# First attention of a two-layer gated decoder: turns by DMA, masks as rows of the keys, three buffers, all steps written out, routing's tables at its end

## The chip, the cores and the metric

The kernel runs on one core of a Trainium2 chip. The metric is the device time of one execution in microseconds; less is better. The core has TensorE (matmuls and the loading of their weights), VectorE, ScalarE, GpSimd and SP, which here only issues transfers, and 16 DMA engines. The profile calls them PE, DVE, ACT, POOL and SP.

## The reference

32 sequences of 256 tokens with 256 channels pass two layers. Each is a gated cross-attention to 120 context rows and a gated feed-forward part; the first layer's is a mixture of 8 experts with the best 2 per token.

```python
x = x + jnp.tanh(g_xattn[0]) * _L0_xattn_ref(_layernorm(x, axis=-1), ctx_1024, L0_xattn_Wq, L0_xattn_Wkv, L0_xattn_Wo, L0_xattn_bo)
x = x + jnp.tanh(g_ffn[0]) * _L0_ffn_ref(_layernorm(x, axis=-1), L0_ffn_w_router, L0_ffn_w1, L0_ffn_w2, L0_ffn_w3)
...
            q = _apply_rope(q)
            k = _apply_rope(k)
            attn = jnp.einsum('bhqd,bhkd->bhqk', q, k) * scale
            attn = jax.nn.softmax(attn, axis=-1)
            out = jnp.einsum('bhqk,bhkd->bhqd', attn, v)
            out = out.transpose(0, 2, 1, 3).reshape(B, Nq, C)
            return out @ Wo + bo
...
        scores = jax.nn.softmax(xf @ w_router.T, axis=-1)
        expert_weights, expert_indices = jax.lax.top_k(scores, K)
        h = jax.nn.silu(jnp.einsum('td,edh->eth', xf, w1)) * jnp.einsum('td,edh->eth', xf, w3)
        y = jnp.einsum('eth,ehd->etd', h, w2)
```

There are 16 heads of 16 channels. The second layer has an attention with layer norms and a gate, and a ternary feed-forward part with a short convolution; the change doesn't touch them.

## The kernel before, in words

Four stages run one after the other, each a block in which every engine has its own program: `attention_first`, which also routes tokens to experts, `experts`, `attention_second` and `ternary_ffn`. Between blocks all engines meet.

`attention_first` takes one sequence (a batch) per step, in a software pipeline: in step n an engine works on batch n - s for the stage s of each piece, and the pieces of a step stand in an order written out by hand. `filled` writes 12 steps out, loops over two steps at a time for the other 20, and writes the drain of 10 steps out. Engines tell each other of progress by semaphores with named steps (`Signal`, `wait`); `freed` waits until a buffer's last reader is through.

A batch goes like this. SP loads xT, x and the context. TensorE makes queries (into `ps_c`) and keys and values (`ps_a`) from high and low halves in bf16. VectorE multiplies with the rotary tables, GpSimd adds (`qf`, `kf`), ScalarE and VectorE write high, high again and low halves side by side, 32 columns each for a pair of heads, into `qx` (two tiles of 128 tokens, 8 pairs, 96 columns) and `kx`. TensorE turns `kx` (L1044, 8 transposes into `ps_b`) and `qx` (L1095 and L1101, 16 into `ps_d` and `ps_b`). ScalarE copies them out: keys twice with a mask that keeps one head of the pair (`k2`, L540 and L543), queries as they are (`q2`, L567 and L569). TensorE then makes the scores of 128 queries to all keys four heads at a time (`ps_m`, the names ms0 to ms7), VectorE takes each maximum (`mneg`), splits it in two halves (`mx`), TensorE turns it (L1086, into `ps_a`), ScalarE copies it (`mt`, L560), and VectorE copies it eight times into rows 96 to 127 of `q2` (L844). Rows 96 to 127 of `k2` hold one-hot rows, so that the score matmuls of the second kind (keys as rows, `ps_e`, sc0 to sc7) come out less the maximum. ScalarE takes the exponentials into `probs`, TensorE multiplies with the values (pv0, pv1), turns the result (tb, oT), VectorE divides, TensorE projects (`ps_b`), and VectorE adds the residual: `x1`, stored by SP.

Routing follows, on the same batch some steps later: norm (`e_xn`, L616, two buffers), a turn and the router's product in fp32, best two, a rank for each token by matmuls with a triangle and with ones, the slot number, and four scatters by GpSimd (L462, L499) of rows into `sent`. The copy of L616 waits until the scatters of the batch two earlier have landed.

The experts' weights are loaded in six pieces; ScalarE casts (`high`, L210) and VectorE subtracts (`low`, L216). Four pieces are done between steps 1 to 8 of `attention_first`, two at the start of `experts`.

`experts` begins with a count of tokens (L2110), VectorE's tables from it, and SP's eight stores of zeros behind each expert's rows (L1868); then SP loads rows by tiles of 256 (L1880), ScalarE and VectorE split them, a DMA transpose turns them (L1885, 128x1024 bf16), and TensorE starts (L2107).

## Time and profile before

| | us |
|---|---|
| median of 3 runs | 1959.78 |
| lowest, highest | 1959.65, 1960.63 |
| the profiled execution | 1951.88 |
| its span | 1950.1 |
| mean granted clock of TensorE in it | 0.959 of full speed |

All durations come from the profiled execution. Line numbers in the rows are those of the kernel before. Times of matmuls overlap their successors a little, so that the distance between starts tells more than a duration. Idle time in brackets names who ended it.

### The profile page before, as it was taken

The numbers are of one execution on the slowest core, as the hardware profiler recorded it, in microseconds if no ns is written. First come the engines' busy times: TensorE is split into PE (matmuls) and PEld (weight loads), VectorE is DVE, ScalarE is ACT, GpSimd is POOL, SyncE is SP. The second block draws the span as 40 slices with busy tenths as digits, with TensorE's granted clock in tenths as the row PEclk, the third lists the DMA queues.
The fourth block names the chain that finished last, engine by engine and source line by source line (L and its number), as shares of the span: only waits on it lengthen the run. The fifth ranks groups of instructions, "written<-read, shape, count | busy, mean of one in ns | idle before, by whom it ended". The sixth has DMA issues, their size and how long they took to land. (4 is left out here: it accounts for less than half of the span.)

```text
span 1950.1 us, 52076 instructions
## 1 busy us (share of the span) xinstructions
PE 1707.9 (88%) x15841; PEld 1433.9 (74%) x15841; DVE 1489.0 (76%) x4340; ACT 1418.6 (73%) x2824; POOL 1003.7 (51%) x1295
## 2 busy tenths in 40 slices
PE   4989999999719999999975999999999578888887
PEld 3667888888518999999963888888887366666666
DVE  4879999999534354433325999999998699999996
ACT  6888999999524454444424777777777499999997
POOL 3448888888622333333337667666661233333332
PEclk8899999999959999999987999999999799999999
DMA  5434343342229675555524555555541112211111
GB/s 177 162 106 151 114 129 114 119 130 87 89 96 218 146 135 143 138 137 138 139 74 94 109 127 112 119 117 118 123 111 53 62 55 65 65 62 59 61 59 51
DMA packets 265532, 212.75 MB, mean 109 GB/s; under 512 B 108160, under 2 KB 255104, under 8 KB 264384
## 3 DMA queue, kind: packets, MB, share of 16 engines
q1 hardware_dynamic: 240832, 176.50, 32.3%
q0 software_dynamic: 24576, 34.62, 8.6%
q8 instruction: 75, 1.23, 0.3%
...
## 5 line engine op out<-in xcount | busy, mean ns | idle before, releaser
L2107 PE MATMUL e_ps_ab<-e_turned,k_w_hi 128*128 128x256 bf16 (+1 forms) x1704 | 285.1, 274 | 21.6 <-DMA e_turned<-e_rows 21.6
L1929 POOL TENSOR_TENSOR e_h_lo<-e_h 128x256 bf16<-128x256 f32 (+1 forms) x213 | 139.0, 653 | 303.4 <-DVE e_h L2046 303.4
L2046 DVE TENSOR_TENSOR e_h<-e_s,e_ps_ab 128x256 f32<-128x256 f32 (+1 forms) x213 | 88.2, 415 | 227.6 <-ACT e_s L1954 227.6
L2107 PE MATMUL e_ps_ab<-e_turned,k_w_lo 128*128 128x256 bf16 (+1 forms) x852 | 233.1, 274 | 0.0
L2107 PEld LDWEIGHTS e_ps_ab<-e_turned,k_w_hi 128*128 (+1 forms) x1704 | 177.6, 107 | 36.3 <-issue 21.7
L1954 ACT ACTIVATE e_s<-e_ps_ab 128x256 f32<-128x256 f32 (+1 forms) x213 | 81.1, 382 | 123.9 <-PE e_ps_ab L2107 122.9
L2489 PE MATMUL f_ps_h<-f_qh,p_arena 128*128 128x256 bf16 x512 | 122.8, 279 | 35.5 <-DVE f_ql L2453 28.2
L1961 ACT ACTIVATE e_yo<-e_ps_y,e_xe 128x256 f32<-128x256 f32 x142 | 59.5, 470 | 112.7 <-PE e_ps_y L2107 112.7
L2489 PE MATMUL f_ps_h<-f_ql,p_arena 128*128 128x256 bf16 x512 | 122.0, 278 | 0.0
L2107 PE MATMUL e_ps_y<-e_w_hi,e_h 128*128 (+1 forms) x426 | 116.5, 273 | 0.0
L1289 POOL DMA_INDIRECT a_xa<-back_rows,a_where x64 | 107.9, 1686 | 15.7 <-issue 15.2
L2107 PE MATMUL e_ps_y<-e_w_hi,e_h_lo 128*128 (+1 forms) x426 | 115.9, 272 | 0.0
L2107 PE MATMUL e_ps_y<-e_w_lo,e_h 128*128 (+1 forms) x426 | 115.7, 272 | 0.0
L2267 POOL TENSOR_TENSOR f_y<-f_y,f_tmp 128x510 f32<-128x510 f32 x32 | 43.6, 1362 | 136.6 <-DVE f_y L2388 136.6
L1299 POOL DMA_INDIRECT a_xa<-back_rows,a_where x64 | 100.4, 1568 | 21.4 <-issue 21.0
L2107 PEld LDWEIGHTS e_ps_ab<-e_turned,k_w_lo 128*128 (+1 forms) x852 | 90.7, 107 | 7.0
L2489 PEld LDWEIGHTS f_ps_h<-f_qh,p_arena 128*128 128x128 bf16 x512 | 50.7, 99 | 61.4 <-DVE f_ql L2453 35.9
L2039 DVE TENSOR_TENSOR e_rows<-e_xe,e_rows 128x256 bf16<-128x256 f32 x142 | 78.2, 589 | 19.4 <-ACT e_rows L1948 19.1
L499 POOL DMA_INDIRECT sent_rows<-k_xn,k_slot x64 | 71.2, 1112 | 18.6 <-issue 18.6
L506 POOL TENSOR_TENSOR a_qf<-p_arena 128x512 f32<-128x512 f32 x32 | 40.7, 1273 | 62.8 <-DVE p_arena L674 62.8
L462 POOL DMA_INDIRECT sent_rows<-k_xn,k_slot x64 | 64.0, 1000 | 17.0 <-issue 17.0
L889 PE MATMUL a_ps_b<-a_wo,a_ot 128*128 128x256 f32 x256 | 64.6, 398 | 0.6 <-ACT a_ot L578 0.6
(429 smaller groups left out, 6421.7 us busy)
## 6 DMA issues: line engine op xcount, KB each, us to landing
...
```

What stands on the lines that cost most here:

```text
L462: nc.gpsimd.indirect_dma_start(sent[:, :], bass.IndirectOffsetOnAxis(ap=slot[:, b.par, t, 0:1], axis=0), e_xn[:, b.par, t, :], None).then_ ...
L499: nc.gpsimd.indirect_dma_start(sent[:, :], bass.IndirectOffsetOnAxis(ap=slot[:, b.par, t, 1:2], axis=0), e_xn[:, b.par, t, :], None).then_ ...
L889: last = nc.tensor.matmul(dst, l, r, start=(n == 0), stop=(n == len(terms) - 1))
L1289: nc.gpsimd.indirect_dma_start(xa[:, b.par, t, :], None, y_rows[:, :], bass.IndirectOffsetOnAxis(ap=where[:, b.par, 2 * t + 1:2 * t + 2], ...
L1299: nc.gpsimd.indirect_dma_start(xa[:, b.par, t, :], None, y_rows[:, :], bass.IndirectOffsetOnAxis(ap=where[:, b.par, 2 * t + 0:2 * t + 1], ...
L1929: nc.gpsimd.tensor_tensor(h_lo[0:k, b.par, c, :], h[0:k, b.par, c, :], h_hi[0:k, b.par, c, :], ALU.subtract).then_inc(mg.sem, 1)
L1954: nc.scalar.activation(s[0:k, b.par, c, :], ps_ab[0:k, bank(b, c), 0:N], ACT.Silu).then_inc(ma.sem, 1)
L1961: nc.scalar.activation(yo[:, b.par, t, :], ps_y[:, b.par, t * D:(t + 1) * D], ACT.Copy, scale=xe[:, b.n % XE, t, D:D + 1]).then_inc(my.sem, 1)
L2039: last = nc.vector.tensor_tensor(rows_[:, b.n % XR, 1, :, t, :], xe[:, b.n % XE, t, 0:D].rearrange("p (k n) -> p k n", k=KC), rows_[:, b.n ...
L2046: nc.vector.tensor_tensor(h[0:k, b.par, c, :], s[0:k, b.par, c, :], ps_ab[0:k, bank(b, c), N:2 * N], ALU.mult).then_inc(mh.sem, 1)
L2107: last = nc.tensor.matmul(to, left, right, start=(i == 0), stop=(i == len(terms) - 1))
L2489: last = nc.tensor.matmul(dst, l, r, start=(n == 0), stop=(n == len(terms) - 1))
```

## The change

- `unrolled` writes all 45 steps out (14 stages), with `Staged` for the waits, whose values are constants.
- `kx` and `qx` become 128 columns wide per head and per pair. Each head's keys are written to their own columns, the other head's stay zero, and the one-hot part is stored once in columns 96 to 127 (`own`). SP turns them with one DMA transpose each per batch (128x2048 bf16) straight into `k2` and `q2`, which get three buffers; `v1` too. The transposes on TensorE, ScalarE's four copies out of them and the masks are gone.
- The maxima are spread into `q2` by a DMA from SP (`m_ld`) instead of VectorE's copy.
- `e_xn`, `slot` and `pair` have four buffers.
- The four pieces of weights of `attention_first` are cast and subtracted in steps 32 to 36.
- The count, the tables and the stores of zeros stand at the end of `attention_first`; SP and ScalarE issue four stores each. `experts` no longer has them.
- The order of each engine's pieces is another. GpSimd's operations are the same.

The diff, cut to its core:

```diff
+def arrived(eng, sems, batch, parts=1):
+
+    if batch is not None:
+        eng.wait_ge(sems[batch.n % len(sems)], 16 * parts * (batch.n // len(sems) + 1))
...
-        self.slot = sb("slot", [P, 2, NT, 2], mybir.dt.int32)
+        self.xn = sb("xn", [P, 4, NT, WIDE])
+        self.slot = sb("slot", [P, 4, NT, 2], mybir.dt.int32)
...
+class Staged:
+
+
+
+    def __init__(self, sem, steps):
+        self.sem = sem
+        self.steps = [(name, int(stage)) for name, stage in (s.split(":") for s in steps.split())]
+        assert len(set(self.steps)) == len(self.steps)
+
+    def value(self, n, step):
+
+        names = [name for name, _stage in self.steps]
+        place = names.index(step)
+        when = n + self.steps[place][1]
+        return sum(min(B, max(0, when - stage + (i <= place))) for i, (_name, stage) in enumerate(self.steps))
+
+    def wait(self, eng, batch, step):
+
+        if batch is not None:
+            eng.wait_ge(self.sem, self.value(batch.n, step))
...
+def unrolled(step, stages, also):
 
 
     def at(n):
-        return lambda s: Batch(n - s, (n - s) // 2, (n - s) % 2) if 0 <= n - s < B else None
-
-    def within(batch):
-        return lambda s: batch.back(s) if s else batch
-
-    for n in range(fixed):
+        return lambda s: Batch(n - s, (n - s) // 2, (n - s) % 2, (n - s) // 4, (n - s) % 4) if 0 <= n - s < B else None
+
+    for n in range(B + stages - 1):
         step(at(n))
         also(n)
-    with eng.Fori(0, (B - fixed) // 2) as k:
-        step(within(Batch(2 * k + fixed, k + fixed // 2, 0)))
-        step(within(Batch(2 * k + fixed + 1, k + fixed // 2, 1)))
...
         xt = pre.arena[:, 5120:6144].rearrange("p (t k n) -> p t k n", t=2, k=KC)
-        qx = sb("qx", [P, NT, NP, 96], BF16)
-        kx = sb("kx", [P, NP, 96], BF16)
-        q2 = sb("q2", [P, 2, NP, N], BF16)
-        k2 = sb("k2", [P, 2, H, S], BF16)
-        v1 = sb("v1", [P, 2, H, VW], F32)
...
+        qx = sb("qx", [P, NP, NT, P], BF16)
+        kx = sb("kx", [P, H, P], BF16)
+        q2 = sb("q2", [P, 3, NP, N], BF16)
+        k2 = sb("k2", [P, 3, H, P], BF16)
+        v1 = sb("v1", [P, 3, H, VW], F32)
...
+        def pad(eng, first, stop):
+
+            sh.s_tab.wait(eng, once, "padding")
+            for e in range(first, stop):
+                at = eng.value_load(sh.padding[0:1, e:e + 1], min_val=0, max_val=E * ROOM - ROWS)
+                eng.dma_start(sent[bass.ds(at, ROWS), :].rearrange("(t p) d -> p t d", p=P), sh.zeros[:, :, :]).then_inc(sh.s_pad, 16)
+
...
+        def own(at):
+
+            rows_ = kx[0:S, :, :]
+            return bass.AP(rows_.tensor, rows_.offset + at, [rows_.ap[0], [2 * P, NP], [P + HD, 2], [1, HD]])
...
+                if b is not None:
+                    act1.wait(sp, b, "k_hi2")
+                    dve1.wait(sp, b, "k_lo")
+                    nc.sync.dma_start_transpose(k2[:, b.n % 3, :, :], kx[:, :, :].rearrange("p h k -> p (h k)")).then_inc(k_ld[b.n % 3], 16)
...
+                if b is not None:
+                    act6.wait(sp, b, "mt")
+                    nc.sync.dma_start(q2[96:128, b.n % 3, :, :], mt[:, :].unsqueeze(1).to_broadcast([2 * H, NP, N])).then_inc(m_ld[b.n % 3], 16)
...
+                    act1.wait(sp, b, "q_hi2")
+                    dve1.wait(sp, b, "q_lo")
+                    nc.sync.dma_start_transpose(q2[:, b.n % 3, :, :].rearrange("p c (t n) -> p (c t) n", t=NT),
+                                                qx[:, :, :, :].rearrange("p c t k -> p (c t k)")).then_inc(q_ld[b.n % 3], 16)
...
-                if n in (4, 5):
-                    sh.load(sp, a, n - 2)
+                if n in (33, 34):
+                    sh.load(sp, a, n - 31)
                 if n == 6:
                     for j in range(SPARE // ROWS):
                         at = E * ROOM + j * ROWS
                         sp.dma_start(sent[at:at + ROWS, :].rearrange("(t p) d -> p t d", p=P), sh.zeros[:, :, :]).then_inc(sh.s_spare, 16)
-                if n in (9, 10):
-                    sh.load(sp, a, n - 5)
+                if n in (37, 38):
+                    sh.load(sp, a, n - 33)
+                if n == STAGES + LAST - 1:
+                    pad(sp, 0, E // 2)
...
+                    arrived(act, k_ld, at(5))
+                    nc.scalar.activation(own(0), kf[0:S, :].rearrange("p (c j d) -> p c j d", j=2, d=HD), ACT.Copy).then_inc(act1.sem, 1)
...
+                    dve7.wait(act, b, "enm")
+                    arrived(act, e_sent[1], at(14), NT)
...
-                if n in (1, 2):
-                    sh.high(nc, n - 1, sh.flat[0])
-                if n in (6, 7):
-                    sh.high(nc, n - 4, sh.flat[1])
+                if n in (32, 33):
+                    sh.high(nc, n - 32, sh.flat[0])
+                if n in (35, 36):
+                    sh.high(nc, n - 33, sh.flat[1])
+                if n == STAGES + LAST - 1:
+                    pad(act, E // 2, E)
...
-                    nc.vector.tensor_copy(q2[96:128, b.par, :, :], mt[:, :].unsqueeze(1).to_broadcast([2 * H, NP, N])).then_inc(dve2.sem, 1)
...
-                if n in (2, 3):
-                    sh.low(nc, n - 2, sh.flat[0])
-                if n in (7, 8):
-                    sh.low(nc, n - 5, sh.flat[1])
+                if n in (32, 33):
+                    sh.low(nc, n - 32, sh.flat[0])
+                if n in (35, 36):
+                    sh.low(nc, n - 33, sh.flat[1])
+                if n == LAST + 11:
+                    tables()
...
+                    arrived(pe, k_ld, b)
+                    arrived(pe, q_ld, b)
+                    for j in range(2):
+                        last = nc.tensor.matmul(ps_m[:, 1, j * 2 * S:(j + 1) * 2 * S].rearrange("p (j s) -> p j s", s=S), q2[0:96, b.n % 3, 2 + j, 0 * P:1 * P],
+                                                k2[0:96, b.n % 3, 4 + 2 * j:6 + 2 * j, 0:S],
+                                                start=True, stop=True)
...
+                if n == LAST + 13:
+                    gp2.wait(pe, final, "eseen")
+                    dve5.wait(pe, final, "top2")
+                    nc.tensor.matmul(ps_m[:, 0, 0:E], ones[:, :], seen[:, :], start=True, stop=True).then_inc(sh.s_count, 1)
+
...
-            s_tab.wait(sp, once, "padding")
-            for e in range(E):
-                at = sp.value_load(padding[0:1, e:e + 1], min_val=0, max_val=E * ROOM - ROWS)
-                sp.dma_start(block_of(at), zeros[:, :, :]).then_inc(s_pad, 16)
             s_tab.wait(sp, once, "row")
             sp.wait_ge(sh.s_spare, 16 * (SPARE // ROWS))
-            sp.wait_ge(s_pad, 16 * E)
+            sp.wait_ge(sh.s_pad, 16 * E)
             for k in range(2):
-                for par in range(2):
-                    sp.wait_ge(sh.sent[k][par], 16 * NT * (B // 2))
+                for quad in range(4):
+                    sp.wait_ge(sh.sent[k][quad], 16 * NT * (B // 4))
```

TensorE, steady step, before: the turn of the maxima (L1086), the turns of queries (L1095, L1101), keys and values, then the scores less the maximum (L1114).

```order
428 L1086 MATMUL a_ps_a<-a_identb,a_mx 32x128 x2
429 L1095 MATMUL a_ps_d<-a_identb,a_qx 96x128 x8
430 L1101 MATMUL a_ps_b<-a_identb,a_qx 96x128 x8
431 L889 MATMUL a_ps_a<-a_wkvh,a_ch 120x512
432 L889 MATMUL a_ps_a<-a_wkvl,a_ch 120x512
433 L889 MATMUL a_ps_a<-a_wkvh,a_cl 120x512
434 L889 MATMUL a_ps_a<-a_wkvh,a_ch 120x512
435 L889 MATMUL a_ps_a<-a_wkvl,a_ch 120x512
436 L889 MATMUL a_ps_a<-a_wkvh,a_cl 120x512
437 L1114 MATMUL a_ps_e<-a_q,a_k 120x256 x2
```

TensorE, steady step, of the change: the same turn (L1143), the first two pairs of maxima of the next batch (L1150, L1162) around the context's turn, keys and values, the rank, the projection (`a_wo`), and the scores (L996).

```order
1417 L1143 MATMUL a_ps_a<-a_identb,a_mx 32x128 [waits a0_act1,a0_dve5]
1418 L1143 MATMUL a_ps_a<-a_identb,a_mx 32x128
1419 L1150 MATMUL a_ps_m<-a_k,a_q 128x240 [waits a0_q_ld0,a0_k_ld0]
1420 L1150 MATMUL a_ps_m<-a_k,a_q 128x240
1421 L973 MATMUL a_ps_d<-k_ident,a_of 128x128 [waits a0_dve7]
1422 L973 MATMUL a_ps_d<-k_ident,a_of 128x128 x3
1423 L1162 MATMUL a_ps_m<-a_k,a_q 128x240 x2
1424 L963 MATMUL a_ps_a<-a_wkvh,a_ch 120x512 [waits a0_act6,a0_gp2]
```

```order
1433 L1179 MATMUL a_ps_c<-k_seen,k_ones 128x8 x2
1434 L963 MATMUL a_ps_b<-a_wo,a_ot 128x256 [waits a0_act6]
1435 L963 MATMUL a_ps_b<-a_wo,a_ot 128x256 x3
1436 L996 MATMUL a_ps_e<-a_q,a_k 120x256 [waits a0_act6,a0_m_ld2]
1437 L996 MATMUL a_ps_e<-a_q,a_k 120x256
```

The query turns are gone, and between the turn of the maxima and the scores that need it stand more products than before, with a wait for the spreading transfer (`m_ld`) at the scores and one for both turns (`q_ld`, `k_ld`) at L1150.

SP, steady step, before: store of x1, slots, then the four loads.

```order
94 L414 DMA x_rows<-a_x 128x2x256
95 L57 ISA
96 L398 ISA
97 L398 DMA slots<-k_slot 128x4
98 L57 ISA
99 L402 ISA
100 L402 DMA p_arena<-in_xT 128x512
101 L57 ISA
102 L404 DMA a_xa<-in_x 128x2x256
103 L57 REGISTER_ALU
```

SP, steady step, of the change, from the spread of the maxima (L449) to the next one.

```order
228 L449 DMA a_q<-a_mt 32x8x256
229 L453 DMA x_rows<-a_x 128x2x256
230 L458 DMA_TRANSPOSE a_q<-a_qx 128x16x128
231 L463 DMA p_arena<-in_xT 128x512
232 L467 DMA slots<-k_slot 128x4
233 L433 DMA_TRANSPOSE a_k<-a_kx 128x16x128
234 L437 DMA a_xr<-in_x 128x2x256
235 L441 DMA a_xa<-in_x 128x2x256
236 L445 DMA a_ca<-in_ctxT 128x240
237 L449 DMA a_q<-a_mt 32x8x256
```

Three transfers have come in among the six, two of them turns, and register and branch instructions are gone.

## Rows read from the trace of the kernel before

**Rows 1.** By stretch: us, busy us of PE, PEld, DVE, ACT, POOL, clock, DMA share, GB/s.

```profile
540.00:600.00 60.00, 17.35 (x119) 14.79 (x120) 22.41 (x70) 14.64 (x25) 15.34 (x25) 0.56 0.41 112
420.09:434.43 14.34, 14.34 (x147) 11.59 (x146) 13.74 (x55) 14.05 (x29) 11.97 (x17) 1.00 0.39 115
```

**Rows 2.** Timeline of TensorE, one step: start us, us, engine, line, operation, tiles, count.

```profile
420.09 0.29 PE L1086 MATMUL a_ps_a<-a_identb,a_mx 128*32 128x128 bf16 x2
420.30 0.65 PE L1095 MATMUL a_ps_d<-a_identb,a_qx 128*96 128x128 bf16 x8
...
421.23 0.38 PE L889 MATMUL a_ps_a<-a_wkvh,a_ch 128*120 128x512 bf16 x1
...
422.53 0.38 PE L1114 MATMUL a_ps_e<-a_q,a_k 128*120 128x256 bf16 x2
...
426.15 1.90 PE L889 MATMUL a_ps_b<-a_wo,a_ot 128*128 128x256 f32 x8
...
429.45 0.58 PE L1044 MATMUL a_ps_b<-a_identb,a_kx 120*96 120x120 bf16 x8
429.94 0.38 PE L1050 MATMUL a_ps_m<-a_k,a_q 96*128 96x240 bf16 x2
```

**Rows 3.** Timeline of TensorE, the turn of the maxima: first, ninth, last batch.

```profile
43.23 0.27 PE L1086 MATMUL a_ps_a<-a_identb,a_mx 128*32 128x128 bf16 x2
...
176.35 0.28 PE L1086 MATMUL a_ps_a<-a_identb,a_mx 128*32 128x128 bf16 x2
...
503.36 0.28 PE L1086 MATMUL a_ps_a<-a_identb,a_mx 128*32 128x128 bf16 x2
```

**Rows 4.** Groups by line, 300 to 400 us: busy us, mean ns | idle before.

```profile
L540 ACT ACTIVATE a_k<-a_ps_b,a_pairmask 96x960 bf16<-96x960 bf16 x7 | 7.5, 1073 | 0.0
L567 ACT ACTIVATE a_q<-a_ps_d 96x1024 bf16<-96x1024 bf16 x7 | 7.0, 1000 | 0.0
L560 ACT ACTIVATE a_mt<-a_ps_a 32x256 bf16<-32x256 bf16 x7 | 2.6, 372 | 1.8 <-PE a_ps_a L1086 1.8
L844 DVE COPY a_q<-a_mt 32x2048 bf16<-32x2048 bf16 x7 | 6.5, 926 | 3.0 <-ACT a_mt L560 3.0
L504 POOL TENSOR_TENSOR a_rstd<-a_ve,a_half 128x2 f32<-128x2 f32 x7 | 7.3, 1039 | 0.2
L479 POOL TENSOR_TENSOR a_e_rstd<-a_e_ve,a_half 128x2 f32<-128x2 f32 x7 | 5.1, 722 | 0.0
L499 POOL DMA_INDIRECT sent_rows<-k_xn,k_slot x14 | 15.8, 1129 | 3.3 <-issue 3.3
```

**Rows 5.** A stretch with one turn; a small transfer with its landing, 300 to 400 us.

```profile
818.00:820.00 2.00, 2.00 (x20) 1.78 (x19) 0.00 (x0) 0.84 (x2) 0.54 (x1) 1.00 0.72 139
...
slots<-k_slot SPq DMA_DIRECT2D x7, 2.0 KB, 1.7
```

**Rows 6.** The two lines that cast and subtract weights: ns min/median/max, first and last.

```profile
L210 ACT ACTIVATE k_w_hi<-k_w_f x4: 2533/2554/2602, 27.5 to 115.9; 128x2816 bf16<-128x2816 f32 x4
L210 ACT ACTIVATE e_w_hi<-k_w_f x2: 2746/2754/2763, 566.4 to 569.1; 128x3072 bf16<-128x3072 f32 x2
...
L216 DVE TENSOR_TENSOR k_w_lo<-k_w_f,k_w_hi x4: 3081/3358/4039, 47.2 to 147.0; 128x2816 bf16<-128x2816 f32 x4
```

**Rows 7.** The drain: ScalarE's group, then TensorE's and SP's timelines, with releasers.

```profile
L616 ACT ACTIVATE k_xn<-a_x,a_e_nmr,a_e_rstd 128x256 f32<-128x256 f32 x8 | 4.4, 592 | 15.0 <-DMA sent_rows<-k_xn,k_slot 15.0
...
566.46 0.17 PE L2110 MATMUL e_ps_y<-k_seen,k_ones 128*128 128x8 bf16 x1 [12.19 <-PEq L240]
588.26 0.61 PE L2107 MATMUL e_ps_ab<-e_turned,k_w_hi 128*128 128x256 bf16 x2 [21.63 <-DMA e_turned<-e_rows]
...
568.10 9.32 SPq L1868 DMA_DIRECT2D sent_rows<-k_zeros  x8
580.44 2.70 SPq L1880 DMA_DIRECT2D e_xe<-sent_rows  x3
584.91 1.36 SPq L1885 DMA_TRANSPOSE e_turned<-e_rows  x1
```

1207 lines of the change are left out of this document (575 added, 632 removed).

## The prediction

> **What bounds the kernel now.** I read the stages first: in the stretch from 540 to 600 us, between the first attention and the experts, TensorE is busy for 17.35 of 60 us at a mean granted clock of 0.56, while in one step of the first attention (420.09 to 434.43) it is busy for all of its 14.34 us at clock 1.00 [rows 1]. In that step ScalarE is busy for 14.05, VectorE for 13.74 and GpSimd for 11.97 us, and the DMA engines for 0.39 of it, 5.6 us [rows 1]. So the steady part is bound by TensorE, with two engines close behind, and the end of the stage is bound by waits.
>
> Next the timeline of TensorE over that step, from one turn of the maxima (L1086) to the next [rows 2]: there is no idle entry in it. Then the times of the same matmul for the first, ninth and last batch: 43.23, 176.35 and 503.36 [rows 3]. From the ninth on, 23 intervals take 327.0 us, 14.22 each; the first eight take 133.1, 16.6 each. The start is slower than the steady part although its steps hold less work.
>
> **The change, part by part.**
>
> *1. Turns by DMA: TensorE.* The 16 matmuls that turn queries begin at 420.30 and the next product begins at 421.23: 0.93 us. The 8 that turn keys take 429.45 to 429.94: 0.49 us [rows 2]. TensorE loses 1.42 us of 14.34, and nothing is added to it; its floor becomes **12.92 us** per step.
>
> *2. The other engines.* ScalarE loses four copies out of the turns (two of queries, 1.00 each, and two of keys with the mask, 1.07 each, of which one row each stands here): 4.1 us, so its floor is 14.05 - 4.1 = 9.9 [rows 1, 4]. VectorE loses the copy that spreads the maxima (L844), 0.93 us busy and 3.0/7 = 0.43 idle ahead of it [rows 4]: 13.74 - 0.93 = 12.81. GpSimd changes in order alone: 11.97 busy plus the pause ahead of its scatters, 3.3 us in 7 steps and the same for the second pair, 0.94 together: 12.91 [rows 1, 4]. Writing all steps out also removes the register instructions that the order of before shows between VectorE's operations; I price them at nothing, since VectorE's floor already lies under TensorE's.
>
> GpSimd's power on 128x2 (L504) takes 1.04 us where it starts beside VectorE's spreading copy, and the same shape elsewhere (L479) 0.72 [rows 4]. If the copy is what holds it, GpSimd's floor falls to 12.6. The Trainium skill (SBUF — State Buffer, "Who interferes with whom") says that a VectorE copy in a two-port mode and a GpSimd operation exclude each other for the whole instruction; by it the 0.3 us come back, without it they don't. The forecast doesn't need them.
>
> *3. What DMA gets.* In the experts' stage one turn of 128x1024 bf16 lies alone in a window of 2.00 us, with a DMA share of 0.72: 1.44 us of all 16 engines [rows 5]. The change issues two of 128x2048 per step, so 4 x 1.44 = 5.8 us. The spreading of the maxima (32 rows of 8 x 512 B, 128 KB) has no row; it is bounded below by nothing and above by a 128 KB turn, 0.7, and I take 0.5, near the turn since its pieces are small too. Sum: 5.6 + 5.8 + 0.5 = **11.9 us** of DMA work per step. That lies under 12.92, but it is 90% of it. The Trainium skill (DMA: Bandwidth & Descriptors, "Latency and other measured facts") gives 261 GB/s for DMA transposes; by it the two would take 4.0 us and the sum would be 10.1. The window gives 182 GB/s, and the sum goes by the window.
>
> SP waits in its order. Behind the maxima's spread stand the store of x1, the query turn, the next xT, the slots, the key turn and three loads; behind a query turn that waits for q_lo, all of the rest. The turns are asked for on TensorE one to two steps later and have three buffers, so only the spread is close to the path.
>
> *4. The spread.* Before: maxima turned, ScalarE copies, VectorE copies, scores. Now a transfer stands in VectorE's place. A 2 KB transfer takes 1.7 us from issue to landing here [rows 5]; I take 2.2 for 128 KB, bounds 1.7 to 4. With ScalarE's copy of 0.37 (L560) [rows 4] and two hand-overs of 0.1 the chain is 2.8 us after the turn. TensorE's work in between, by the new order and the times of [rows 2]: two maxima pairs 0.4, the context turn 0.4, keys and values 421.23 to 422.53 = 1.3, the projection about 1.7 (1.90 with the last one's tail): 3.9 us. So it is hidden with **1.1 us** to spare. With a landing of 4 us it would cost 0.7 per step.
>
> *5. The steady step.* Three floors of 12.92, 12.91 and 12.81 in one chain of waits won't meet without friction. Before, the second engine was at 98% and TensorE still had no gap. I take **13.2 us**, from 12.95 to 14.3 (the time of before, if DMA sets the pace).
>
> *6. The expert weights* (four casts of 2.55 us on ScalarE, four subtractions of 3.36 us on VectorE [rows 6]) leave steps 1 to 8 for steps 32 to 36. In the first eight intervals they hold 10.2 and 13.4 us of engines that are nearly full: taking both out at face value gives 133.1 - 23.6 = 109.5, and the shorter step 8 x 1.14 = 9.1 less: 100.4. **Gain 32.7** (bounds: 13.4 + 9 = 22 if only VectorE's count, 36). Two copies of masks at the very start go too, and two turns of longer latency stand in the first batch's way; I take these as equal. In steps 32 and 33 two subtractions lie in nearly full steps of VectorE: 6.7 us are paid there; the two at 35 and 36 fall into steps with no query work, and these are some 3 us shorter as they are now. The rest: 23 x 13.2 + 6.7 - 3 = 307.3 against 327.0. **Gain 19.7.**
>
> *7. The drain.* From the last turn of maxima (503.36) to the experts' first instruction (566.46) 63.1 us pass [rows 3, 7]. ScalarE's normalisation waits 15.0 us there for scattered rows whose two buffers are not free [rows 7]. With four buffers that wait has no cause; the spread's latency and the one more stage of scores cost 1 us. **Gain 14** (bounds 6, if GpSimd's four scatters a batch are next in line, to 22).
>
> *8. Tables and padding.* Now: count at 566.46, eight padding stores from 568.10 over 9.32 us, first load at 580.44, first turn at 584.91, first product at 588.26: 21.8 us [rows 7]. Afterwards count, tables and padding are done when the stage ends. What is late next are the last weights: two casts of 2.75 (to 5.5), then the second subtraction of 3.36 behind the first, 2.75 + 2 x 3.36 = 9.5 [rows 6], the rows' low half 0.8, and turn to product 588.26 - 584.91 = 3.35: 13.6. **Gain 8.2.** If the loads are late instead, up to 3 less. ScalarE and VectorE run the second half of these in before too, hidden by the wait for padding, whose cover is now gone.
>
> Sum: 32.7 + 19.7 + 14 + 8.2 = 74.6 us. The profiled execution took 1951.88 (span 1950.1), which gives 1877.3; the median of the three runs is 1959.78, 7.9 above it, and against that the forecast is **1885 us**.
>
> **The rivals.**
>
> *A. DMA or SP sets the pace.* 11.9 us of work at 90% leaves no room for bunching, and scatters of GpSimd share the engines. For it: the share is the highest in the kernel. Against it: all loads have a step's slack. Then the step is some 14.3: 31 x 1.1 = 34 more, 1919.
>
> *B. Slower than before: the turns are dear.* The new ones are twice as wide as the one measured. If a 128x2048 turn took longer than twice the 128x1024 one, the step would be 6.1 + twice that. The gain of 74.6 is gone at 74.6 / 31 = 2.4 us per step above 13.2, that is 4.8 us for a turn in place of 2.88. At 5.8 the step is 17.7 and the kernel takes 1885 + 31 x 4.5 = 2025. Against it: a wider turn is more blocks of the same size.
>
> *C. The floors are met and the drain collapses.* Step 12.95, drain gain 22: 1885 - 31 x 0.25 - 8 = 1869.
>
> *D. The start isn't shortened.* If the first steps were long from latencies and not from the weights, 22 us of the 32.7 stay: 1907. Against it: the intervals come down to 14.3 just when the weights are done.
>
> **How the numbers follow.** Forecast (1875 to 1900) 0.60; A 0.17; D 0.07; C 0.11; B 0.05. The range has to leave out at most 0.2: from **1865**, under C, to **1920**, which takes in D and A. About 0.2% (4 us) is what a measurement of this kernel can tell from no change. Faster by more than that: all but B and a worse A, **0.93**; within it 0.02; slower 0.05.
>
> **What would show it.** In the profile after: the interval between two turns of maxima in the steady part 13.0 to 13.6 and TensorE without idle entries there (parts 1, 5); ScalarE near 75% of it (2); DMA share near 0.9 in it (3); no wait of the scores for the transfer of maxima (4); the ninth turn of maxima near 143 and the last near 450 (6); last turn to the experts' first instruction near 49 (7); from there to the first product near 14 (8). Wrong would be: TensorE idle at each step for a_q or a_k from DMA (A, B), a turn's landing over 5 us, or a first product after 530.

## The result and the profile after

The changed kernel takes 1937.39 us (median; 1934.98 to 1938.79), the kernel before 1959.72 in the same comparison: a ratio of 0.9885 with a 95% interval of 0.9868 to 0.9902. It is faster by 22 us, where 75 were forecast, and the time lies above the range of 1865 to 1920. The profiled execution took 1934.98 us (span 1933.2) where the sum gave 1877.3.

First the places that the prediction's steps end at: the turn of the maxima (L1143 here, L1086 before) for the first, ninth and last batch, then the experts' first instruction and the first product. All rows are of the timeline of the changed kernel, and answer to [rows 3] and [rows 7].

```profile
45.48 0.40 PE L1143 MATMUL a_ps_a<-a_identb,a_mx 128*32 128x128 bf16 x2
...
149.96 0.29 PE L1143 MATMUL a_ps_a<-a_identb,a_mx 128*32 128x128 bf16 x2
...
496.55 0.28 PE L1143 MATMUL a_ps_a<-a_identb,a_mx 128*32 128x128 bf16 x2 [0.91 <-DVE a_mx L871]
...
557.19 2.76 ACT L229 ACTIVATE e_w_hi<-k_w_f 128x3072 bf16<-128x3072 f32 x1 [15.83 <-PEq L273]
...
570.53 0.61 PE L2115 MATMUL e_ps_ab<-e_turned,k_w_hi 128*128 128x256 bf16 x2 [29.35 <-DMA e_turned<-e_rows]
```

| Stretch | before | forecast | after | forecast missed by |
|---|---|---|---|---|
| to the first turn | 43.2 | 43.2 | 45.5 | 2.3 |
| first 8 intervals | 133.1 | 100.4 | 104.5 | 4.1 |
| other 23 intervals | 327.0 | 307.3 | 346.6 | 39.3 |
| last turn to the experts | 63.1 | 49.1 | 60.6 | 11.5 |
| experts' start to first product | 21.8 | 13.6 | 13.3 | -0.3 |
| first product to the end | 1361.8 | 1361.8 | 1362.7 | 0.9 |

So 39 of the 58 us are in the steady part, which was to become shorter by 20 us and became longer by 20; another 11.5 are in the drain. That the kernel is faster at all, as forecast, comes from the start (28.6 us) and from the experts' first product (8.5), not from the step.

The second view compares two steps of the changed kernel by windows (columns: length, then busy time and instructions of TensorE, its weight loads, VectorE, ScalarE, GpSimd, then the granted clock, the DMA share and GB/s). The first step lies ahead of the first scatter of rows, the second is one of the 19 alike (15.06 to 15.08 us); the last four of the 23 intervals take 18.15, 15.85, 13.37 and 12.95.

```profile
122.35:135.39 13.04, 13.04 (x123) 10.37 (x123) 13.00 (x54) 10.73 (x24) 9.55 (x15) 1.00 0.88 204
330.78:345.85 15.07, 13.60 (x123) 10.20 (x123) 14.61 (x55) 10.91 (x26) 11.66 (x17) 1.00 0.76 194
```

In the first, TensorE is busy throughout, in 13.04 us: within what part 5 forecast (13.2, from 12.95). In the second VectorE is busy for 14.61 us, 1.61 more, with the same instructions but one, and TensorE for 13.60 of 15.07. The DMA share is the lower one in the longer step. TensorE's longest wait in the second step, 0.7 us, is for VectorE's maxima, and none is for a transfer. So the step is VectorE's, and its groups by line for 300 to 400 us (busy us, mean ns, then the idle time ahead) name the instructions:

```profile
L789 DVE SCALAR_TENSOR_TENSOR a_pair<-a_e_ex,a_tg,a_e_rec 128x4 f32<-128x4 f32 x7 | 9.5, 1351 | 0.0
L809 DVE COPY k_xn<-a_pair 128x2 f32<-128x2 f32 x6 | 6.5, 1085 | 0.0
L890 DVE SCALAR_TENSOR_TENSOR a_qx<-a_qf,a_rstd,a_qx 128x256 bf16<-128x256 f32 x14 | 6.1, 474 | 0.0
```

Two instructions on 4 and 2 elements per partition lead the list, ahead of everything with 256 or 512 elements. The timelines of VectorE and of GpSimd, in the step ahead of the scatters (first three rows) and in a steady one (the others), show when they are long:

```profile
125.94 1.06 DVE L760 TENSOR_TENSOR a_kx<-a_kf,a_kx 120x256 bf16<-120x256 f32 x1
...
128.09 0.16 DVE L789 SCALAR_TENSOR_TENSOR a_pair<-a_e_ex,a_tg,a_e_rec 128x4 f32<-128x4 f32 x1
...
129.63 0.16 DVE L809 COPY k_xn<-a_pair 128x2 f32<-128x2 f32 x1
...
306.86 1.36 DVE L789 SCALAR_TENSOR_TENSOR a_pair<-a_e_ex,a_tg,a_e_rec 128x4 f32<-128x4 f32 x1
...
309.61 1.08 DVE L809 COPY k_xn<-a_pair 128x2 f32<-128x2 f32 x1
...
305.93 0.96 POOL L555 DMA_INDIRECT sent_rows<-k_xn,k_slot  x1 [0.30 <-issue]
306.91 1.29 POOL L560 TENSOR_TENSOR a_qf<-p_arena 128x512 f32<-128x512 f32 x1
...
309.50 1.16 POOL L512 TENSOR_TENSOR a_xl<-p_arena,a_xh 128x512 bf16<-128x512 f32 x1
```

`pair` ends (308.22) with GpSimd's addition `a_qf` (308.20), the copy (310.69) with GpSimd's subtraction `a_xl` (310.66). They cost 1.20 and 0.92 us more than alone, 2.12 together. VectorE's busy time grows by less, 1.61, mainly because `a_kx`, which takes 1.06 us beside `a_qf` in the step without scatters, takes 0.41 in the steady one: the 13.04 us hold such a meeting too, and that 2.12 lies so near to 15.07 - 13.04 = 2.03 is in part chance. Before the change the same `pair` took 0.20 us and the same copy 0.16. GpSimd's scatters shift its additions to this place: without them `a_qf` starts at 125.44, 2.65 us ahead of `pair`, and with them it follows the scatter of 305.93 at once. The meeting then comes back in each of the 19 steps.

The Trainium skill (SBUF — State Buffer, "Who interferes with whom") says that a VectorE instruction with two SBUF inputs contends with a GpSimd instruction that reads SBUF, that a copy in a two-port mode does too, that whoever comes second is fully blocked for the whole instruction, and that a reduction never contends on trn2. By that, a 0.16 us operation can cost the length of GpSimd's. The rows agree in that both end with GpSimd's operation. They don't show who came second: the record of `pair` begins 0.05 us ahead of that of `a_qf`. Experiments e1, e3 and e4 test the moment, e2 the kind of operation, and that for the copy alone: `pair` was moved but never exchanged.

### The profile page after: what moved, and what is told of

Its sections match the earlier page's. It is cut to its first block and busy times, and to the rows that moved or that the text cites. A ratio compares the mean times of both kernels' runs of the same rounds, so it can differ in the third digit from the quotient of the medians.

```text
span 1933.2 us, 48348 instructions
## 1 busy us (share of the span) xinstructions
PE 1676.1 (87%) x15073; PEld 1385.0 (72%) x15073; DVE 1508.7 (78%) x4308; ACT 1310.5 (68%) x2695; POOL 1000.9 (52%) x1297
## 5 line engine op out<-in xcount | busy, mean ns | idle before, releaser
L519 POOL DMA_INDIRECT sent_rows<-k_xn,k_slot x64 | 64.2, 1003 | 23.3 <-issue 23.0
L555 POOL DMA_INDIRECT sent_rows<-k_xn,k_slot x64 | 62.2, 973 | 19.7 <-issue 18.9
L2496 PE MATMUL f_ps_y<-p_arena,f_zq 128*128 128x256 bf16 x512 | 61.1, 273 | 1.2 <-ACT f_zq L2339 1.2
```

The source lines that it names most:

```text
L519: nc.gpsimd.indirect_dma_start(sent[:, :], bass.IndirectOffsetOnAxis(ap=slot[:, b.quad, t, 0:1], axis=0), e_xn[:, b.quad, t, :], None).the ...
L555: nc.gpsimd.indirect_dma_start(sent[:, :], bass.IndirectOffsetOnAxis(ap=slot[:, b.quad, t, 1:2], axis=0), e_xn[:, b.quad, t, :], None).the ...
L2496: last = nc.tensor.matmul(dst, l, r, start=(n == 0), stop=(n == len(terms) - 1))
```

## Experiments

The ratios are to before on the same chip. The step is the mean of the 18 intervals between the 10th and the 28th turn of maxima. The kernel before takes 1955.4, 1959.1, 1959.7, 1969.1 and 1970.3 us in the five sets of runs, the changed one 1937.4 and 1935.5 in the two that hold it. The step and first product of before are those of its one trace, of an execution of 1951.88 us.

| Kernel | step, us | ratio to before, or time | first product, us |
|---|---|---|---|
| before | 14.34 | 1 | 588.3 |
| changed | 15.07 | 0.9885; 0.9907 when repeated | 570.5; 571.0 |
| e1: `pair` elsewhere | 14.02 | 1920.6 of 1970.3 | 554.9 |
| e2: copy as reduction | 14.14 | 1923.4 of 1970.3 | 556.9 |
| e3: `pair` and copy elsewhere | 14.03 | 0.9729 | 549.3 |
| e4: before, copy elsewhere | 15.62 | 1983.8 of 1970.3 | 619.3 |
| e5: e3 and four value buffers | 13.81 | 0.9730 | 545.9 |
| e9: e5 and copies as reductions | 13.48 | 0.9744 | 540.7 |
| e11: e9 and a second store | 13.5 | 1906.9 of 1959.1 | 538.4 |

**e1: one instruction moved.** The edit, in VectorE's order:

```
 nc.vector.tensor_reduce(total[:, :], e_ex[:, :, :], AX_X, ALU.add)
+nc.vector.reciprocal(e_rec[:, :], total[:, :])
+nc.vector.scalar_tensor_tensor(pair[:, b.quad, :, :], ...)
 nc.vector.tensor_reduce(mneg[:, 0, 12:16], ...)
-nc.vector.reciprocal(e_rec[:, :], total[:, :])
 nc.vector.reciprocal(rsum[:, 1, :], ...)
-nc.vector.scalar_tensor_tensor(pair[:, b.quad, :, :], ...)
```

> The changed kernel with two of VectorE's routing instructions (the reciprocal e_rec and the weights' product pair, 128x4) in another place of VectorE's order: directly behind the sum total, where VectorE has an idle 0.45 us and GpSimd issues scatters. Nothing is added or left out. Theory (shared SBUF access): pair took 1.36 us beside GpSimd's 128x512 addition a_qf and 0.16 where nothing ran beside it; at the new place it takes 0.16 to 0.22, the step falls from 15.07 by up to 1.2, to 13.9 to 14.1, and the copy into k_xn stays at 1.0 to 1.1 if its phase stays. Rival 1 (DMA sets the pace of 15.07, its share being 0.80): the step stays at 15.0 to 15.1. Rival 2 (the lost time only moves to the next two-input operation that meets GpSimd): the step stays above 14.7 and another short VectorE operation takes over 1 us.

Measured: step 14.02, time 1920.6. The groups of VectorE for 300 to 400 us:

```profile
L780 DVE SCALAR_TENSOR_TENSOR a_pair<-a_e_ex,a_tg,a_e_rec 128x4 f32<-128x4 f32 x7 | 1.6, 223 | 0.2
L809 DVE COPY k_xn<-a_pair 128x2 f32<-128x2 f32 x8 | 1.4, 177 | 0.0
```

`pair` fell as expected, and the step with it. The copy fell too, which I had not expected: it wasn't moved, presumably since it now meets GpSimd at another moment; that was not tested. DMA as the pace (rival 1) is excluded: the same transfers now fit in 14.0 us.

**e2: same place, another operation.**

```
-nc.vector.tensor_copy(e_xn[:, b.quad, :, D:D + 1], pair[:, b.quad, :, 0:1])
+nc.vector.tensor_reduce(e_xn[:, b.quad, :, D:D + 1], pair[:, b.quad, :, 0:1], AX_X, ALU.add)
```

> The changed kernel with one instruction exchanged at its own place: the weight's copy into k_xn (128x2) that stands between two maxima (L809) is made by a reduction over one element instead of a copy; same input, same output, same order. Theory (the copy locks with GpSimd because of its access mode, a reduction doesn't): the instruction takes 0.16 us in place of 1.08, pair stays at 1.36, and the step falls by 0.9 to 14.1 to 14.3. Rival (any VectorE operation at that place waits, because of what it reads or because its turn comes late): it stays at 1.0 and the step at 15.07.

```profile
L789 DVE SCALAR_TENSOR_TENSOR a_pair<-a_e_ex,a_tg,a_e_rec 128x4 f32<-128x4 f32 x8 | 10.6, 1328 | 0.0
...
L809 DVE TENSOR_REDUCE k_xn<-a_pair 128x2 f32<-128x2 f32 x7 | 1.0, 139 | 0.0
```

At the same place of the order, with the same operands, the reduction takes 139 ns where the copy took 1085; `pair` is untouched at 1328. The step is 14.14, 0.93 shorter. So it is the kind of operation and not the place alone. That the copy runs in a two-port mode is the page's reason; no trace shows the mode.

**e3: both moved.** As e1, with the copy right behind `pair`.

> The changed kernel with the reciprocal e_rec, pair and the copy into k_xn all directly behind the sum total in VectorE's order. Nothing is added or left out. Theory: both long instructions fall to 0.16 to 0.22 us, VectorE's work per step to 12.9 and the step from 15.07 to 13.0 to 13.3; over the 22 steady intervals and some of the others this is 40 to 46 us, so the kernel takes 1890 to 1900 us against 1937.4 (0.965 to 0.970 of before). Rival 1 (DMA or SP sets the pace): 1930 to 1940. Rival 2 (the loss moves on): 1915 to 1935, with another VectorE operation over 1 us.

The ratio is 0.9729 (0.9713 to 0.9746); `pair` takes 222 and the copy 169 ns; the first product comes 21 us earlier. But the step is 14.03, as in e1, and not 13.0 to 13.3. The theory's cause holds, but it promised 2 us per step and got 1.04: the copy alone is worth 0.93 (e2) and both together hardly more, so that something else stands at 14.0. In the timelines of TensorE, VectorE and ScalarE in e3 another thing is late:

```profile
315.08 1.05 PE L1128 MATMUL a_ps_e<-p_arena,a_v 120*32 120x256 f32 x16
...
315.56 0.47 DVE L717 TENSOR_TENSOR a_k_sin<-a_ps_a,p_arena 120x128 f32<-120x128 f32 x2
...
317.15 0.38 ACT L597 ACTIVATE a_v<-a_ps_a 120x256 f32<-120x256 f32 x1 [2.23 <-PE a_ps_e L1128]
```

ScalarE's copy of the values waits for these two alone, the later of which ended at 316.13, and it starts 1.02 us after that. TensorE's turn of maxima waits for this copy.

**e4: the collision put into the kernel before.** The kernel before with its 0.16 us copy moved by one VectorE instruction:

```
-nc.vector.tensor_copy(e_xn[:, b.par, :, D:D + 1], pair[:, b.par, :, 0:1])
 nc.vector.tensor_tensor(k_cos[0:S, :], ps_a[0:S, 0:D], cos[0:S, 0, :], ALU.mult)
+nc.vector.tensor_copy(e_xn[:, b.par, :, D:D + 1], pair[:, b.par, :, 0:1])
 (the two products of k_sin)
```

> The kernel before with one instruction in another place: the weight's copy into k_xn (L853, 0.16 us, which starts at 351.36, just ahead of GpSimd's a_qf at 351.52 to 352.75) now stands behind the first product of the keys' rope, at about 351.76, inside a_qf. Nothing is added or left out. Theory (shared SBUF access): the copy takes 0.9 to 1.0 us, and since VectorE's 13.74 of 14.34 us become 14.5, the step grows from 14.22 to 14.4 to 14.8, the kernel by 4 to 15 us. Rival (the long copies of the changed kernel come from its DMA queues or from their place between maxima): the copy stays at 0.16 to 0.2 and the time within 2 us of before.

Its group for 300 to 400 us, then one step of it beside GpSimd's:

```profile
L865 DVE COPY k_xn<-a_pair 128x2 f32<-128x2 f32 x6 | 6.7, 1122 | 0.0
...
322.88 1.27 POOL L506 TENSOR_TENSOR a_qf<-p_arena 128x512 f32<-128x512 f32 x1 [0.59 <-DVE p_arena L674]
...
323.05 1.12 DVE L865 COPY k_xn<-a_pair 128x2 f32<-128x2 f32 x1
```

The long copy appears in a kernel that has none of the change: no DMA turns, two buffers, its own order. With one tiny copy 0.4 us later in the order the step is 1.28 us longer than in the trace of before, where I expected 0.2 to 0.6. Not all of that is the copy, whose excess is 0.96: `a_kx` (L744, two inputs in SBUF) takes 900 ns in e4 and 411 before, and ends with GpSimd's `a_e_ve`: it looks like a further meeting that the new phase brings. The size has a second caveat. The kernel is 13 us slower than before beside it (one run, above all seven of before, 1966.5 to 1972.3), but its first product comes 31 us later than in the trace of before, which is of an execution some 18 us faster than those seven. That the copy grows is shown; how much of 1.28 us is the move's is not. So the copy's part of the cause is shown from two sides: e2 by the kind of operation, e4 by the moment.

**e5: the wait for the values.** e3 with `v1` in four buffers, so that ScalarE waits for a product that is one batch older.

```
-v1 = sb("v1", [P, 3, H, VW], F32)
+v1 = sb("v1", [P, 4, H, VW], F32)
-pe9.wait(act, at(7), "pv1")
+pe9.wait(act, at(8), "pv1")
```

> The kernel of e3_both_early with four buffers for the values a_v in place of three, so that ScalarE's copy a_v (L597) waits for a product of values one batch older, long finished. Nothing is left out. In e3_both_early this copy starts 0.6 to 1.2 us after TensorE's last product of values and 0.8 to 1.5 after VectorE's k_sin, while in the short steps before 136 us it starts 0.07 after the product; the step there is 14.0 against 13.4. Theory (the wait for TensorE's product of values is what is late): the copy starts 0.1 us after k_sin, TensorE's idle time ahead of the turn of the maxima goes, and the step falls to 13.1 to 13.6; the kernel by 10 to 20 us against e3_both_early. Rival 1 (the copy is late for something that the semaphores don't show): it stays 0.8 to 1.5 after k_sin and the step at 14.0. Rival 2 (DMA, busy for 0.88 of that step, is the floor): the copy comes earlier and the step stays at 13.9 to 14.0.

The copy now starts 0.09 us after `k_sin` in all steady steps but one, where it is 0.38; mean step 13.81, between the two theories. The first product is 3.5 us earlier than in e3, but the time is the same (1915.99 us; 0.9730, 0.9713 to 0.9746). Windows over three of its steps:

```profile
286.80:300.50 13.70, 13.20 (x122) 10.31 (x121) 12.93 (x54) 10.73 (x24) 11.61 (x18) 1.00 0.84 217
313.90:328.90 15.00, 13.19 (x123) 10.31 (x121) 14.90 (x55) 10.84 (x24) 11.52 (x18) 1.00 0.81 201
342.95:356.90 13.95, 13.17 (x122) 10.28 (x121) 12.70 (x54) 10.73 (x24) 11.61 (x17) 1.00 0.96 211
```

The step of 15.00 is a collision once more. In the timelines of VectorE and GpSimd:

```profile
319.23 1.89 DVE L785 COPY k_xn<-a_pair 128x2 f32<-128x2 f32 x1
...
318.83 0.96 POOL L555 DMA_INDIRECT sent_rows<-k_xn,k_slot  x1 [0.30 <-issue]
319.82 1.27 POOL L560 TENSOR_TENSOR a_qf<-p_arena 128x512 f32<-128x512 f32 x1
```

Here the copy's record begins 0.59 us before `a_qf` and ends with it (321.12 and 321.09). In the other 19 steps between 150 and 420 us the copy starts 0.09 to 0.14 us after the same scatter (L555) does and takes 0.17; here it starts 0.40 after it and lasts through the rest of the scatter and the whole addition. So a scatter's issue on GpSimd may hold a copy too, and the loss can be more than one operation of GpSimd; one row shows that, and no run tests it. The change of order had moved the copy into a gap, and the gap doesn't always fit.

**e9: both copies as reductions.** e5 with both copies into `k_xn` made by reductions, as in e2.

> The kernel of e5_values_four (routing's weights behind the sum, four buffers for the values) with both copies into k_xn made by a reduction over one element, as in e2. Nothing is left out. In e5 the step varies between 13.5 and 15.0 us, and in the long one the copy took 1.89 us behind GpSimd's a_qf. Theory (what is left above 13.4 are such meetings of copies with GpSimd): no VectorE operation of under 0.3 us takes over 0.6, the steps come down to 13.4 to 13.6, and the kernel takes 5 to 8 us less than e5 (0.969 to 0.971 of before). Rival (DMA at a share of 0.89 to 0.96 is what is left): mean step 13.6 to 13.8 as in e5, the time within 3 us of it.

```profile
200.00:400.00 200.00, 197.09 (x1798) 152.17 (x1797) 198.44 (x792) 162.17 (x357) 171.07 (x253) 1.00 0.92 217
...
L785 DVE TENSOR_REDUCE k_xn<-a_pair 128x2 f32<-128x2 f32 x8 | 1.3, 157 | 0.3
L867 DVE TENSOR_REDUCE k_xn<-a_pair 128x2 f32<-128x2 f32 x7 | 1.0, 141 | 0.0
```

In 200 us TensorE (197.09) and VectorE (198.44) are nearly always busy: the state that part 5 of the prediction described. The steady intervals read 13.41 but for two of 14.7 and three within 0.4 of it. The two long ones are again such a meeting, of other operations. `a_qx` takes 1.25 us for its two in the usual step and here 2.32, beside GpSimd's `a_cl` and `a_xb`, and TensorE then waits 1.28 us for VectorE:

```profile
257.69 2.32 DVE L890 SCALAR_TENSOR_TENSOR a_qx<-a_qf,a_rstd,a_qx 128x256 bf16<-128x256 f32 x2
```

The kernel takes 1903.49 us, against 1935.46 for the changed kernel beside it: 32 us less, and faster than both given kernels. Its ratio to before, 0.9744 (0.9716 to 0.9771), doesn't tell it from e3 and e5, which stood on other chips; the expected 0.969 to 0.971 was missed. What separates them is the trace: step (13.48 for 14.03 and 13.81) and first product.

**The changed kernel repeated**, as the measure beside e9:

> The changed kernel itself once more, as the measure for the runs beside it, since they are compared with before on one chip and not with it. Nothing is left out. Expected: the ratio to before of its first measurement, 0.987 to 0.990, a step of 15.07 us, and a_pair and the copy into k_xn at 1.3 and 1.1 us each, since their meeting with GpSimd's additions is set by the order and not by chance.

Ratio 0.9907 (0.9879 to 0.9934), time 1935.46 of 1955.38, step 15.07, `pair` 1414 and the copy 1085 ns. The collision is in the order and comes back in another set of runs, with the same step to 0.01 us.

**e11: more work for DMA.** e9 with each store of x1 made twice (0.6 us more of SP's issue, 256 KB more a step).

> The kernel of e9_three_edits with the store of x1 (256 KB a batch) made a second time, into rows that nobody reads: 0.6 us more of issue on SP and some 0.9 us more work for the DMA engines a step, whose share there is 0.91. Nothing is left out. Theory (in e9 the step of 13.41 is TensorE's and VectorE's, and DMA still has slack): the step stays under 13.6 and the kernel within 5 us of e9. Rival (DMA's 0.91 is in truth full, as rival A of the prediction had it for its 0.90): the step grows by 0.5 to 1.0, to 13.9 to 14.4, and the kernel by 10 to 25 us.

The window of 200 to 400 us:

```profile
200.00:400.00 200.00, 197.72 (x1796) 152.33 (x1796) 193.79 (x790) 158.82 (x356) 170.12 (x253) 1.00 1.02 238
```

The step stays at 13.5 (the intervals read 13.43 to 13.56 in the steady part) and the first product comes at 538.4. At a DMA share of 1.02 and 238 GB/s the engines wait for transfers three times in these 200 us, 0.9 us together, and the usual interval is 13.45 for 13.41. So neither in e9 at 0.92, nor in the changed kernel at 0.76, does DMA set the pace. The whole time is 1906.9 of 1959.1, one run on another chip than e9's 1903.5: within the 5 us of the theory, outside the rival's 10 to 25.

**e6: the weights' work at the start again.** Part 6 alone undone: casts and subtractions in steps 2, 3, 5 and 6.

```
-if n in (32, 33):
-    sh.low(nc, n - 32, sh.flat[0])
-if n in (35, 36):
-    sh.low(nc, n - 33, sh.flat[1])
+if n in (2, 3):
+    sh.low(nc, n - 2, sh.flat[0])
+if n in (5, 6):
+    sh.low(nc, n - 3, sh.flat[1])
 (the same for sh.high and sh.load)
```

> The changed kernel with part 6 alone undone: the four casts and four subtractions of the experts' weights run in steps 2, 3, 5 and 6 of the first attention again instead of 32, 33, 35 and 36, the loads earlier to match. Theory (parts 6 of the prediction holds): the ninth turn of maxima comes at 165 to 175 us instead of 150, the four intervals that held the subtractions at the end fall by 3, 3, 1 and 1 us, and the kernel is 10 to 20 us slower than the changed one. Rival (the start got shorter from the direct transfers or the three buffers, not from the weights): the ninth turn stays within 5 us of 150 and the kernel within 5 us.

Ninth turn, last turn and first product in e6, then in the changed kernel repeated:

```profile
167.77 0.29 PE L1143 MATMUL a_ps_a<-a_identb,a_mx 128*32 128x128 bf16 x2
...
506.33 0.28 PE L1143 MATMUL a_ps_a<-a_identb,a_mx 128*32 128x128 bf16 x2 [0.85 <-DVE a_mx L871]
...
578.70 0.60 PE L2115 MATMUL e_ps_ab<-e_turned,k_w_hi 128*128 128x256 bf16 x2 [28.84 <-DMA e_turned<-e_rows]
```

```profile
151.90 0.28 PE L1143 MATMUL a_ps_a<-a_identb,a_mx 128*32 128x128 bf16 x2
...
497.55 0.28 PE L1143 MATMUL a_ps_a<-a_identb,a_mx 128*32 128x128 bf16 x2 [1.04 <-DVE a_mx L871]
...
571.01 0.60 PE L2115 MATMUL e_ps_ab<-e_turned,k_w_hi 128*128 128x256 bf16 x2 [29.42 <-DMA e_turned<-e_rows]
```

The weights' work costs 15.9 us by the ninth turn and saves 7.1 from there to the last; with 1.1 us of drain, 7.7 are left at the first product. Of the 15.9, 8.9 lie ahead of the first turn (55.35 for 46.43), where e6 does three casts and two subtractions; before the change only two casts lay there (27.47 and 37.73). So e6 prices the placing in steps 2 to 6 and not exactly that of before. Of the whole time one run (1945.06 of 1969.06, 0.988) can't show so little; by the traces the lower end of my 10 to 20 us was missed.

**e7: three row buffers.** Rows, slots and weights in three buffers in place of four.

> The changed kernel with three buffers for the normalised rows, their slots and weights in place of four (before had two). Nothing is left out. In the drain of the changed kernel ScalarE's normalisation still waits 1.87 and 4.32 us for scattered rows. Theory 1 (the buffers decide the drain): with three it waits 5 to 10 us more in all and the stage's end comes 5 to 10 us later. Theory 2 (GpSimd's four scatters of a batch, 5.6 us of it in order, are what the rows wait for, whichever buffer they take): the waits move, and the stage's end comes within 2 us of the changed kernel's.

I expected 5 to 10 us; it took 2120.4, some 185 us more. Against the changed kernel repeated 155.5 of them lie ahead of the last turn of maxima and 29.2 between it and the first product. The windows of 200 to 400 us, and ScalarE's waits for 300 to 400 (us in total, times, longest):

```profile
200.00:400.00 200.00, 146.81 (x1170) 118.69 (x1162) 128.53 (x511) 105.15 (x226) 109.57 (x164) 0.83 0.60 136
...
ACT k_xn L632 <- DMA sent_rows<-k_xn,k_slot: 28.6, 4, 7.6
```

The steady step grows to 21 us, since ScalarE waits 7 us in each for the rows. So the fourth buffer is no mere reserve for the drain, as I had it: in the new order a row buffer is held from stage 10 to the landing behind stage 13, and the four are what the steady part needs. Theory 1 had the direction in the drain and nothing of the steady part; theory 2 is excluded.

**e10: more work for GpSimd in the drain.** One more addition of 128x512 in each of the steps 41 to 44:

```
+if 41 <= n <= 44:
+    nc.gpsimd.tensor_tensor(qf[:, :, :], rc[:, :, :], rs[:, :, :], ALU.add)
```

> The changed kernel with one more GpSimd addition of 128x512 (1.27 us, into a tile that nobody reads any more) in each of the steps 41 to 44, that is in the last part of the drain, 5.1 us in all. Nothing is left out. From 532.83 on GpSimd issues 16 scatters in 19.6 us without a pause of over 0.7. Theory (GpSimd's queue of scatters is what the end of the drain waits for): the experts' first instruction comes 4 to 5 us later after the last turn of maxima than 60.6, and so does everything behind. Rival (the chain of latencies through normalisation, router and scatters' landing sets it): 0 to 1.5 us.

From the start of the last normalisation to the end of the last scatter the changed kernel repeated takes 533.68 to 552.81, 19.1 us, and e10 takes 23.1. The rows are ScalarE's and GpSimd's timelines in e10:

```profile
535.65 1.09 ACT L640 ACTIVATE k_xn<-a_x,a_e_nmr,a_e_rstd 128x256 f32<-128x256 f32 x2 [4.33 <-DMA sent_rows<-k_xn,k_slot]
...
557.74 0.96 POOL L556 DMA_INDIRECT sent_rows<-k_xn,k_slot  x1 [0.30 <-issue]
558.73 1.27 POOL L585 TENSOR_TENSOR a_qf<-p_arena 128x512 f32<-128x512 f32 x1
...
562.64 2.76 ACT L229 ACTIVATE e_w_hi<-k_w_f 128x3072 bf16<-128x3072 f32 x1 [17.66 <-PEq L273]
```

Three of the four additions lie ahead of the last scatter, 3.8 us, and it comes 3.9 later; the fourth lies beside its landing. Counted from the last turn of maxima the experts start after 63.8 us for 60.1, 3.7 more, a little under the expected 4 to 5 (and the queue holds 14 scatters from 532.83 on, not the 16 that I wrote). The whole time is 1938.8, one run, 3.3 above the changed kernel beside it. So the last 19 us of the drain are GpSimd's queue.

**e8: the padding stores back in the experts' stage.**

> The changed kernel with the eight padding stores (256 rows of zeros each) issued by SP at the start of the experts' stage, as before, and not by SP and ScalarE at the end of the first attention. Nothing is left out. In the changed kernel GpSimd drains its last scatters 4.5 us after the last one was issued, and before the change the stage ended 2.6 us after it. Theory (the padding stores lie ahead of the last scatters in the DMA engines): the drain shrinks to about 2.5 us, the experts' first instruction comes 2 us earlier (555.2), but SP issues the stores for 9 us and the first product comes 4 to 8 us later than in the changed kernel; the kernel is 2 to 6 us slower. Rival (the drain is the price of the block's end): it stays at 4.5.

```profile
553.20 0.96 POOL L553 DMA_INDIRECT sent_rows<-k_xn,k_slot  x1 [0.30 <-issue]
...
557.07 5.42 ACT L229 ACTIVATE e_w_hi<-k_w_f 128x3072 bf16<-128x3072 f32 x2 [14.08 <-PEq L273]
...
558.07 8.42 SPq L1905 DMA_DIRECT2D sent_rows<-k_zeros  x8
...
576.85 0.60 PE L2114 MATMUL e_ps_ab<-e_turned,k_w_hi 128*128 128x256 bf16 x2 [34.02 <-DMA e_turned<-e_rows]
```

From the last scatter's end to the experts' first instruction: 4.8 us in the changed kernel (552.40 to 557.19), 2.9 here (554.16 to 557.07). So the padding costs 1.9 us ahead of the last scatters' landing, as expected, and saves 6.4 behind: from the experts' start to the first product it is 19.8 us here and 13.4 in the changed kernel repeated. Moving the padding, one piece of part 8, is worth 4.5. The one run of 1943.6 of 1969.1 can't show so little of the whole.

## Why the prediction was wrong

**The step that failed** is number 2, carried into 5: "GpSimd changes in order alone: 11.97 busy plus the pause ahead of its scatters", with VectorE's floor at 12.81. I took the durations of VectorE's instructions as their own and let the order change only waits. But the copy takes 0.16 us alone and 1.08 beside a GpSimd operation on SBUF, and `pair` 0.16 and 1.36. I had the mechanism in view: GpSimd's power (L504, 1.04 us) beside VectorE's copy (L844) in [rows 4], and the Trainium skill's rule beside it. I used it for one known meeting, as a gain of 0.3 us, and didn't ask which new meetings the moved instructions would make. That gain came (the power, now L564, takes 730 ns), and 2.1 us went. VectorE's work is 14.61 and not 12.81; without the two meetings it is what part 2 said, 12.93 in e5's step of 13.70. The 19 alike steps at 1.87 us over the forecast are 35.5 us of that row's 39.3, and the last four intervals, which hold the subtractions, the other 3.8.

The two meetings don't explain all of the 1.87. Without them the step falls by 1.04 (e3). Another 0.55 came only with a fourth buffer for the values and with reductions (e5, e9): the friction of 0.3 in part 5 was too small as well. 13.48 is left where 13.2 stood.

*Part 1* (TensorE 12.92): nearly right; the three intervals ahead of the scatters take 12.90 to 13.04, and TensorE is busy for 13.17 to 13.20 in e5's three steps. ScalarE (part 2, 9.9) is busy for 10.7 to 10.9, which costs nothing here.

*Part 3 and rival A* (DMA 11.9 us a step, 90%): the work was right in the share's own unit (0.76 to 0.81 of 15.07 is 11.5 to 12.2), the fear was not: e11. The Trainium skill's 261 GB/s for DMA transposes with a non-contiguous middle dimension (DMA: Bandwidth & Descriptors, "Latency and other measured facts") would have made the sum 10.1, by estimate, and the trace speaks for the window's 182.

*Part 4* (the spread hidden): right. It lands 2.4 us after its issue (2.2 taken), and no scores wait for it.

*Part 6* (start): 28.6 gained of 32.7 in the first eight intervals; counted from the span's start to the ninth turn it is 24.5 (176.35 to 151.90 in the changed kernel repeated). e6 gives 15.9 of these to the weights' work, where 23.6 stood, which leaves 8.6 for all else, where 9.1 stood. The 23.6 was too much by its own rows: two of the four casts, 5.1 us, ran ahead of the first turn and not in the eight intervals. The price at the end measured 7.1, for 6.7: 4.8 in the two intervals that were priced and 2.3 in the two that were taken as free.

*Part 7* (drain, 14 forecast, 2.5 came): mis-sized in both directions. ScalarE's normalisation of the last batch, in the timelines of before, comes 44.4 us after the last turn, and 36.7 after (533.29): a gain of 7.7, and the wait didn't go:

```profile
547.75 1.09 ACT L616 ACTIVATE k_xn<-a_x,a_e_nmr,a_e_rstd 128x256 f32<-128x256 f32 x2 [4.85 <-DMA sent_rows<-k_xn,k_slot]
...
562.86 0.97 POOL L499 DMA_INDIRECT sent_rows<-k_xn,k_slot  x1 [0.30 <-issue]
```

```profile
533.29 1.09 ACT L632 ACTIVATE k_xn<-a_x,a_e_nmr,a_e_rstd 128x256 f32<-128x256 f32 x2 [4.32 <-DMA sent_rows<-k_xn,k_slot]
...
532.83 1.04 POOL L519 DMA_INDIRECT sent_rows<-k_xn,k_slot  x1 [0.17 <-issue]
...
551.44 0.96 POOL L555 DMA_INDIRECT sent_rows<-k_xn,k_slot  x1 [0.30 <-issue]
```

"With four buffers that wait has no cause" was the false sentence: I counted buffers and not the stages for which one is held (e7). Behind that normalisation 6 scatters are still to be issued before the change (16.1 us to the end of the last) and 13 after it (19.1): the later stages leave a queue on GpSimd, 3.0 us lost, and e10 shows that it sets the end. The padding takes 1.9 more, and 2.2 is what the block's end lost in all (4.8 against 2.6). 7.7 - 3.0 - 2.2 = 2.5. My lower bound of 6 named this queue and was still too high.

*Part 8*: right, 13.3 for 13.6, and by the chain that was named: the casts end at 562.61, the second subtraction at 566.61, the turn is issued at 567.31 and the first product comes 3.2 us later.

**The rivals.** None of them was it. A came nearest in size (a step of 14.3, 1919 us, for 15.07 and 1937) by a cause that e1 and e11 exclude. What was missing was a rival for instructions that grow, and the range would have needed it: two meetings with a whole GpSimd operation cost 2.1 us a step, 48 us in 23. Their kind was in [rows 4], their size was not: there the power grows by 0.3 us.

**Open.** In e3 ScalarE started 1.0 us after TensorE's recorded end, and in e5 VectorE (349.85) and ScalarE (349.93) once both started 1.3 and 1.0 us after the ends of the matmuls that they wait for (348.51 and 348.94). The ends of matmuls are modelled, so TensorE may in truth have been late; no run here separates that from a late signal. In e9 these waits no longer reach TensorE. Why its step is 13.41 and not 13.04 is in part the same kind of meeting: `a_qx` (L890) takes 474 ns on average in the changed kernel and 688 in e9, where GpSimd's `a_cl` starts 0.2 us after it. In the changed kernel `a_cl` starts 0.4 us after it and is itself the longer one, 0.93 us for 0.73. That was read from the traces and not tested.
